# Cross attentions in slots: the first scores one slot sooner, another order in the slots, moves shared anew, fewer waits on TensorE

## The reference, cut to what matters

```python
q = _split_heads(query @ Wq.T + bq)
k = _split_heads(key @ Wk.T + bk)
v = _split_heads(value @ Wv.T + bv)
scores = jnp.einsum('bhqd,bhkd->bhqk', q, k) / jnp.sqrt(jnp.float32(DEPTH))
scores = scores + mask * jnp.float32(-1000000000.0)
weights = jax.nn.softmax(scores, axis=-1)
ctx = jnp.einsum('bhqk,bhkd->bhqd', weights, v)
ctx = ctx.transpose(0, 2, 1, 3).reshape(query.shape[0], -1, D_MODEL)
return ctx @ Wo.T + bo
```

## Time and profile before

| | us |
|---|---|
| median of 3 runs (lowest, highest) | 2327.14 (2322.26, 2331.49) |
| profiled execution, its own time | 2325.12 |
| its span | 2323.3 |
| granted TensorE clock, mean of the span | 0.944 |
| TensorE busy, whole span | 2062.7 (89%) |
| VectorE, ScalarE, GpSimd busy | 1335.3, 1105.0, 459.7 |
| stage D from 1293.87 to 2065.80 (771.93): TensorE, VectorE, ScalarE, GpSimd busy | 741.43, 476.33, 402.31, 214.06 |
| ScalarE's moves (line 636), mean of one | 0.595 |
| VectorE's moves (line 746), mean of one | 0.685 |

### The profile page before, as it was taken

One profiled execution on the slowest core, in us unless ns is written; L12 is line 12 of the kernel. 1 busy time (PEld: TensorE's weight loads), 2 busy tenths in 40 slices (PEclk: granted clock), 3 DMA queues, 4 the chain that ended last, 5 costly groups with the idle time before them and its releaser, 6 DMA issues. The chain is left out here.

```text
span 2323.3 us, 59919 instructions
## 1 busy us (share of the span) xinstructions
PE 2062.7 (89%) x25136; PEld 1575.4 (68%) x25136; DVE 1335.3 (57%) x3546; ACT 1105.0 (48%) x2109; POOL 459.7 (20%) x367
## 2 busy tenths in 40 slices
PE   6999999999999985588997899999999999987874
PEld 4777777777777763267995677777777777764553
DVE  3566666566666656935114366666666666563685
ACT  4555555555554543521333554555455554551681
POOL 3111122221111100210001333222233332200010
PEclk9999999999999997797998999999999999996867
DMA  4111111111111001003653221122111111100000
GB/s 127 30 30 30 30 30 40 39 41 30 30 30 30 7 2 55 1 9 127 218 200 99 53 53 44 45 53 61 44 53 47 52 44 45 31 2 22 1 1 25
DMA packets 68668, 110.93 MB, mean 48 GB/s; under 512 B 14505, under 2 KB 37170, under 8 KB 68402
## 3 DMA queue, kind: packets, MB, share of 16 engines
q1 hardware_dynamic: 68402, 107.10, 15.7%
HBM read 106.04 MB, written 1.05 MB: 46 GB/s over the span
## 5 line engine op out<-in xcount | busy, mean ns | idle before, releaser
L718 DVE CUSTOM_DVE_ANT_0 maps_d<-scores_d,mask_scaled_d 128x512 f32<-128x512 f32 (+1 forms) x512 | 263.5, 571 | 217.3 <-PE scores_d L519 217.3
L718 DVE CUSTOM_DVE_ANT_0 maps_a<-scores_a,no_mask_a 128x512 f32<-128x512 f32 (+1 forms) x512 | 263.5, 571 | 214.0 <-PE scores_a L519 214.0
L529 PE MATMUL turn_a<-const,maps_a 128*128 128x128 f32 (+1 forms) x1664 | 258.7, 282 | 16.5 <-DVE mapsT_a L746 15.7
L529 PE MATMUL turn_d<-const,maps_d 128*128 128x128 f32 (+1 forms) x1664 | 258.8, 282 | 16.2 <-DVE mapsT_d L746 15.4
L636 ACT ACTIVATE mapsT_d<-turn_d 128x512 f32<-128x512 f32 x224 | 129.6, 595 | 231.8 <-PE turn_d L529 231.7
L636 ACT ACTIVATE mapsT_a<-turn_a 128x512 f32<-128x512 f32 x224 | 129.6, 595 | 231.2 <-PE turn_a L529 231.1
L529 PEld LDWEIGHTS turn_a<-const,maps_a 128*128 128x128 f32 (+1 forms) x1664 | 184.0, 142 | 74.2 <-issue 25.1
L529 PEld LDWEIGHTS turn_d<-const,maps_d 128*128 128x128 f32 (+1 forms) x1664 | 184.1, 142 | 74.0 <-issue 25.1
L641 ACT ACTIVATE maps_a<-maps_a,neg_max_a 128x1024 f32<-128x1024 f32 (+1 forms) x256 | 222.5, 953 | 1.9 <-DVE neg_max_a L725 1.9
L641 ACT ACTIVATE maps_d<-maps_d,neg_max_d 128x1024 f32<-128x1024 f32 (+1 forms) x256 | 222.5, 953 | 1.9 <-DVE neg_max_d L725 1.9
L746 DVE COPY mapsT_a<-turn_a 128x512 f32<-128x512 f32 x192 | 129.8, 685 | 76.7 <-PE turn_a L529 76.3
(11 more groups left out here) (412 smaller groups left out, 4396.8 us busy)
## 6 DMA issues: line engine op xcount, KB each, us to landing
w_c<-in_L_ffn_W SPq DMA_DIRECT2D x30, 1024.0 KB, 6.8
raw_a<-in_ctxT SPq DMA_DIRECT2D x48, 512.0 KB, 3.7
raw_d<-in_ctxT SPq DMA_DIRECT2D x48, 512.0 KB, 3.7
mask_scaled_d<-in_mask SPq DMA_DIRECT2D x32, 400.2 KB, 5.4
raw_a<-in_ctxT SPq DMA_DIRECT2D x16, 65.0 KB, 3.0
raw_d<-in_ctxT SPq DMA_DIRECT2D x16, 65.0 KB, 7.0
x<-in_x SPq DMA_DIRECT2D x1, 1024.0 KB, 5.4
Wk_c_b<-in_L_attn_Wk_c SPq DMA_DIRECT2D x1, 1024.0 KB
```

What stands on the lines that cost most here:

```text
L529: ins = nc.tensor.transpose(TP[at % 2][0:r, P * j:P * j + P], maps[g % 2][:, j, P * t:P * t + r], chip.ident)
L718: nc.vector.tensor_tensor_reduce(maps[b][:, j, cols], SC[j][:, 0:w], mf[m % 2][:, cols] if masked else none[:, 0:w], 1.0, NEG, ALU.add, AL ...
```

## The change

It moves the scores of chunk 0 one slot ahead, from slot 0 of half g (for g+1) to slot 12 of half g (for g+2), so the first ones, (1, 0), run before half 0. VectorE's maxima of chunk 0 move with them and wait only until the tiles of the old rows that they overwrite are turned. The sums go from slot 9 to 10, and there before the k unit. The last v unit of a half goes from 12 or 9 to 11. VectorE moves tiles 7 to 10 (BY_DVE), ScalarE the others, with the copies of k and v units of the same slots; ScalarE's exponentials stay behind slot 6 and now stand before its move of tile 11. TensorE leaves out waits where another wait of its list has already covered them.

```diff
--- before.py
+++ after.py
@@ -265,10 +265,12 @@
 
 GROUPS = HALVES * NB
 K_AT = {1: 0, 4: 1, 7: 2, 10: 3}
-V_AT = [{3: 0, 6: 1, 9: 2, 12: 3}, {3: 4, 6: 5, 9: 6}]
-ROUND_AT = {0: 0, 2: 1, 4: 2, 6: 3}
-SUM_AT = 9
-LATE = 7
+V_AT = [{3: 0, 6: 1, 9: 2, 11: 3}, {3: 4, 6: 5, 11: 6}]
+ROUND_AT = {2: 1, 4: 2, 6: 3}
+NEXT_ROUND_AT = KT - 1
+SUM_AT = 10
+BY_DVE = range(7, 11)
+BY_ACT = [t for t in range(KT) if t not in BY_DVE]
 FIRST = [("n", 0, 0), ("n", 0, 1), ("q", 0, 0), ("k", 0, 0), ("k", 0, 1), ("v", 0, 0), ("k", 0, 2), ("v", 0, 1),
          ("v", 0, 2), ("k", 0, 3), ("v", 0, 3), ("v", 0, 4), ("v", 0, 5), ("v", 0, 6), ("q", 1, 0), ("k", 0, 4),
          ("k", 0, 5), ("k", 0, 6), ("k", 0, 7), ("n", 1, 0), ("n", 1, 1), ("q", 0, 1), ("q", 1, 1)]
@@ -292,10 +294,13 @@
 def round_order():
 
     order = [("score", 0, c, j) for c in range(4) for j in range(4)]
+    order += [("score", 1, 0, j) for j in range(4)]
     for g in range(GROUPS):
         for t in range(KT):
             if t in ROUND_AT and g + 1 < GROUPS:
                 order += [("score", g + 1, ROUND_AT[t], j) for j in range(4)]
+            if t == NEXT_ROUND_AT and g + 2 < GROUPS:
+                order += [("score", g + 2, 0, j) for j in range(4)]
             if t == SUM_AT and g:
                 order.append(("sums", g - 1))
     order.append(("sums", GROUPS - 1))
@@ -371,10 +376,10 @@
 
             if at >= 0:
                 g, t = at // KT, at % KT
-                if t < LATE:
-                    eng.wait_ge(moved_act, LATE * g + t + 1)
+                if t in BY_DVE:
+                    eng.wait_ge(moved_dve, len(BY_DVE) * g + t - BY_DVE.start + 1)
                 else:
-                    eng.wait_ge(moved_dve, (KT - LATE) * g + t - LATE + 1)
+                    eng.wait_ge(moved_act, len(BY_ACT) * g + BY_ACT.index(t) + 1)
 
         def key_columns(chunk):
             return slice(BANK * chunk, BANK * chunk + even(chunk))
@@ -486,7 +491,8 @@
             def k_unit(m, k):
 
                 chunk, h, bank = k % 4, k // 4, bank_of(("k", m, k))
-                pe.wait_ge(ctx_ready, 4 * m + chunk + 1)
+                if h == 0:
+                    pe.wait_ge(ctx_ready, 4 * m + chunk + 1)
                 wait_bank(("k", m, k))
                 for c in range(HALVES):
                     cols, outs = key_columns(chunk), slice(P * h, P * h + P)
@@ -497,7 +503,8 @@
             def v_unit(m, u):
 
                 bank = bank_of(("v", m, u))
-                pe.wait_ge(ctx_ready, 4 * m + u // 2 + 1)
+                if m == 0:
+                    pe.wait_ge(ctx_ready, u // 2 + 1)
                 wait_bank(("v", m, u))
                 for t in range(2 * u, min(2 * u + 2, KT)):
                     cols = slice(P * t, P * t + rows(t))
@@ -512,7 +519,8 @@
                 m, h, w = g // 2, g % 2, cross.width(chunk)
                 if chunk == 0:
                     pe.wait_ge(q_ready, m + 2 if m or h else 1)
-                wait_kept(pe, ("k", m, 4 * h + chunk))
+                if g == 0:
+                    wait_kept(pe, ("k", m, 4 * h + chunk))
                 after(pe, score_free, ROUND["score", g, chunk, 0])
                 for j in range(4):
                     own = slice(PW * j, PW * j + PW)
@@ -524,7 +532,8 @@
                 at, r = KT * g + t, rows(t)
                 if t in (0, CUT // P):
                     pe.wait_ge(exp_done, 8 * g + (4 if t == 0 else 8))
-                wait_moved(pe, at - 2)
+                if t and t % 2 == 0:
+                    wait_moved(pe, at - 2)
                 for j in range(4):
                     ins = nc.tensor.transpose(TP[at % 2][0:r, P * j:P * j + P], maps[g % 2][:, j, P * t:P * t + r],
                                               chip.ident)
@@ -543,9 +552,10 @@
                 at, r, m, h = KT * g + t, rows(t), g // 2, g % 2
                 if t == 0:
                     after(pe, out_kept, g)
-                if h == 0 and t % 2 == 0:
+                if h == 0 and t % 2 == 0 and m == NB - 1:
                     wait_kept(pe, ("v", m, t // 2))
-                wait_moved(pe, at)
+                if t % 2 or t == KT - 1:
+                    wait_moved(pe, at)
                 for a in range(2):
                     for j in range(4):
                         ins = nc.tensor.matmul(OUT[PW * j:PW * j + PW, h, T * a:T * a + T],
@@ -593,6 +603,7 @@
                     scores(0, ROUND_BEHIND[unit])
             pe.wait_ge(set_up, 2 if masked else 3)
             pe.wait_ge(project_free, len(FIRST))
+            scores(1, 0)
             for g in range(GROUPS):
                 m, h = g // 2, g % 2
                 for t in range(KT):
@@ -601,12 +612,14 @@
                     turn(g, t)
                     if t in ROUND_AT and g + 1 < GROUPS:
                         scores(g + 1, ROUND_AT[t])
+                    if t == NEXT_ROUND_AT and g + 2 < GROUPS:
+                        scores(g + 2, 0)
+                    if t == SUM_AT and g:
+                        spread_sums(g - 1)
                     if t in K_AT and m + 1 < NB:
                         k_unit(m + 1, 4 * h + K_AT[t])
                     if t in V_AT[h] and m + 1 < NB:
                         v_unit(m + 1, V_AT[h][t])
-                    if t == SUM_AT and g:
-                        spread_sums(g - 1)
                     if t and t % 2 == 0:
                         values(g, t - 2)
                         values(g, t - 1)
@@ -690,7 +703,10 @@
                     keep_v(a, b)
             for g in range(GROUPS):
                 m, h = g // 2, g % 2
-                for t in range(LATE):
+                for t in BY_ACT:
+                    if t == BY_DVE.stop and g + 1 < GROUPS:
+                        for i in range(8):
+                            exp(g + 1, i // 4, i % 4)
                     move(g, t)
                     if t == 0 and g:
                         keep_out(g - 1)
@@ -698,9 +714,6 @@
                         keep_k(m + 1, 4 * h + K_AT[t])
                     if t in V_AT[h] and m + 1 < NB:
                         keep_v(m + 1, V_AT[h][t])
-                if g + 1 < GROUPS:
-                    for i in range(8):
-                        exp(g + 1, i // 4, i % 4)
             keep_out(GROUPS - 1)
 
         @block.vector
@@ -712,8 +725,8 @@
                 if chunk == 0 and j == 0:
                     if masked and g % 2 == 0:
                         dve.wait_ge(mask_ready, m + 1)
-                    after(dve, turned, KT * (g - 1))
                 if j == 0:
+                    after(dve, turned, KT * (g - 2) + min(BANK // P * (chunk + 1), KT))
                     dve.wait_ge(scored, 4 * g + chunk + 1)
                 nc.vector.tensor_tensor_reduce(
                     maps[b][:, j, cols], SC[j][:, 0:w], mf[m % 2][:, cols] if masked else none[:, 0:w], 1.0, NEG,
@@ -797,19 +810,24 @@
             for s in v:
                 nc.vector.memset(s[:, :, 16:32], 1.0).then_inc(set_up, 1)
             dve.wait_ge(bias_ready, BIASES)
+            for j in range(4):
+                largest(1, 0, j)
             for g in range(GROUPS):
                 m, h = g // 2, g % 2
                 for t in range(KT):
-                    if t >= LATE:
+                    if t in BY_DVE:
                         move(g, t)
+                    if t == NEXT_ROUND_AT and g + 2 < GROUPS:
+                        for j in range(4):
+                            largest(g + 2, 0, j)
                     if t in ROUND_AT and g + 1 < GROUPS:
                         for j in range(4):
                             largest(g + 1, ROUND_AT[t], j)
                         if ROUND_AT[t] == 3:
                             negate(g + 1)
-                    if t >= LATE and t in K_AT and m + 1 < NB:
+                    if t in BY_DVE and t in K_AT and m + 1 < NB:
                         keep_k(m + 1, 4 * h + K_AT[t])
-                    if t >= LATE and t in V_AT[h] and m + 1 < NB:
+                    if t in BY_DVE and t in V_AT[h] and m + 1 < NB:
                         keep_v(m + 1, V_AT[h][t])
                     if t == SUM_AT and g:
                         finish(g - 1)
```

## The result

| | before | after |
|---|---|---|
| median (lowest, highest), us | 2327.3 (2322.26, 2331.49), 4 runs | 2234.73 (2226.17, 2235.96), 4 runs |
| profiled execution, its own time; span | 2325.12; 2323.3 | 2235.69; 2233.9 |
| one pair of halves | 51.50 | 48.53 |
| stage A, D: first turn to output projection | 811.14, 811.64 | 764.62, 764.63 |

The ratio is 0.9595, 95% interval 0.9564 to 0.9626: 92.6 us less in medians, 89.4 in the two spans. The forecast was 2238 and a pair of 48.7.

The account below looks back on a forecast made before the run. TensorE's own work and its stalls bound the kernel. Stalls of 2.67 us per pair plus 0.15 of switches gave 2.8, with the ends 88 us over two stages: 2238 us, own range 2225 to 2250, overall 2205 to 2264.

Parts of the forecast that it names:

- Slot 2: Scores of chunk 1 wait for VectorE's maxima of chunk 0, 0.50 us in both halves; 1.00 per pair goes.
- turn 12: Turn 12 waits for VectorE's move of tile 10, queued behind finish; 0.54 + 0.68 = 1.22 us per pair goes.
- the odd half's end: Last three values units, 1.21 us against 0.81, and some 0.05 at the turn before; 0.45 per pair goes.
- the remnant at slot 10: Even half's k unit waits for the copy of slot 9's v unit; about 0.25 us, which stays.
- The switches: Changed order of TensorE's units makes switches between them cheaper; net 0.15 us per pair, bounds 0 and 0.3.
- ScalarE's new work: Moves 11 and 12 and slot 11's v copy, behind the exponentials, end in time by 0.3 us or more.
- The waits left out: 52 TensorE waits per pair, taken as costing 0; upper bound 52 x 51 ns = 2.65 us per pair.
- The equal values units: Two values units take 0.65 us with or without a wait before them, so met waits cost nothing measurable.
- The ends: First and last halves of each stage: 0.5 us less, about 2 gained; stage 43.5 to 44, two stages 88.
- Another wait in each half's place: Rival: ScalarE's queue or the maxima run 0.5 us over in each half; 2268 us, chance 0.12.
- The sums bank: Rival: scores at slot 12 wait for finish's reciprocal to read their bank; slower, 2349 us, chance 0.04.
- The price of the waits: Rival: waits themselves cost TensorE, half the bound, 1.3 us per pair, 40 us more gained; 2198, chance 0.09.

Follow-up runs that it names:

- e3: Kernel before with only the scores of chunk 0 and their maxima moved to slot 12 of the half before; 2285.00 us, ratio 0.9831.
- e4: Changed kernel with the scores of chunk 0 back at slot 0, all else as changed; 2293.03 us, ratio 0.9865.
- e5: Changed kernel with the sums, and so VectorE's finish, back at slot 9; 2312.94 us, ratio 0.9944.
- e6: Changed kernel with move 10 and the k copy of slot 10 given to ScalarE too; 2285.43 us, ratio 0.9826.
- e2: Changed kernel with all 52 left-out waits per pair put back; 2231.45 us, ratio 0.9598.
- e1: Kernel before with only the 52 waits per pair left out; 2316.67 us, ratio 0.9962.
- e10: Changed kernel run once more, nothing altered; 2232.89 us, ratio 0.9594 against the kernel before.
- e11: Kernel before with four more waits, met long ago, ahead of the scores of slot 2; 2322.92 us, ratio 0.9984.

## Why the prediction was right

**The stalls.** All four were read rightly from distances of start to start. Slot 2 (1.00), turn 12 (1.22) and the odd half's end (0.45) went; the remnant at slot 10 stayed at 0.23 where 0.25 was said. e3 and e4 take them away one group at a time; e5 brings a stall at slot 11 back (1.95 a pair, 0.81 and 1.14), through finish in VectorE's queue, as the prediction had it.

**The switches** were the term that was too small: 0.15 a pair was taken, 0.30 came (2.97 less 2.67). Turn 1 to k unit costs 0.36 where the working used the pair of turn and k unit at 1.90, measured 1.84 now, twice a pair: 0.11 of the missing 0.15. Where sums now precede the k unit, the place that the prediction had no row for, nothing was gained: turn 10, sums and k unit took 1.04 in the even half before and after. The rest is hundredths. The stated bounds were 0 and 0.3, so this came at their edge. Over thirty halves that made 43.9 us of a forecast 41.5.

**ScalarE's new work** was covered as said; the single-tile copy took 0.37 and the cover of move 12 was 0.81, where 0.3 or more was said. e6 gives the margin: one move and one copy more is too many by 1.56 in odd halves.

**The waits left out** were taken as free. e2 shows that they are in the changed kernel. In the kernel before they were not quite (e1, 6 to 8 us). The bound of 2.65 us a pair was twice too high, as only 26 of the 52 were instructions (e1). The gain is in the 1.00 of slot 2 already, since it was part of the stall. The equal values units were the right witness for met waits and said nothing on unmet ones. The Trainium skill, "Perfetto Trace Analysis", Sequencer-only Instruction, was weighed for the other end. Its hidden tail shows here only behind an unmet wait (0.09 us more with the 51 ns instruction than without); behind met ones it shows nowhere. Its statement that the profiled time leaves the wait out holds for the row L91 above, which stays at 51 ns with the wait for the maxima unmet, and does not hold for the row L521: 2.9 us for an instruction that holds the same wait and a met one.

**The ends.** From the first turn on, the two stages gave 46.5 and 47.0 us. The forecast had 43.5 to 44 each, 88 in all. Before stage A's first turn 3.3 were lost: 1.07 for scores (1,0), and the rest the start-up, which differs from one execution to another (first turn at 61.89, and at 59.99 in e10). The clock differs there too: from 48 to 60 the granted clock was 0.72 in this profile, and 0.86 in those of the kernel before and of e10; what that costs isn't shown.

93.5 - 3.3, and 0.7 gained between the stages and 1.5 lost behind stage D, is 89.4, the difference of the spans. With the 1.07 of scores (1,0) taken off in each stage, as the forecast did, the stages gave 91.4 for its 88, and 2.0 lost outside them, in no term of the working, brought that back to 89.4: that the time came within 3.3 us of the forecast is in part luck. Half 30 lost most of its wait at slot 2 (turn to scores 0.68 and not 2.43) but waited for ScalarE at values 11, as the prediction had said.

**The rivals.** Another wait in each half's place (2268) did not come; e6 shows its mechanism, ScalarE's queue, alive one move away. The sums bank (2349) did not come either, and no run made it bite: the reciprocal ended 1.05 us ahead. e5 puts finish sooner, so it is the old stall again and not this rival. The price of the waits (2198, 40 us) came at a fifth of that, and only in the kernel before.

## What to carry to other kernels

Compare each step of a repeated pattern, start to start, with the same step where it isn't held up: the sum of the differences forecast the two stages' gain as 88 us where 93.5 came, where idle time alone would have shown two thirds of it. When an engine at half load makes the bound engine wait, look for the one long piece of work in its queue ahead of the short urgent one, and move the long one behind; here undoing that order costs 80 us, 9 of them by the clock, and ScalarE's own block of 7 us set how much it could take over. Waits that are met cost nothing measurable on TensorE in these kernels; drop or regroup them only ahead of a stall that can't be removed.

## What the runs showed of the hardware that was not expected

- From the release to the first matmul TensorE took 0.15 us when the unmet wait was an instruction of its own ahead of a weight load with another wait, 0.10 when that instruction carried two waits and the load had one (e11), 0.06 when the load itself carried it (e1). The 51 ns of an instruction of its own ran behind the release in the first case.
- The profiled time of such an instruction can hold its wait: 2.77 to 3.30 us in e11, while it was 51 ns for the same wait in the kernel before.
- The granted clock fell to 1.2 GHz for 3.4 us, three times a stage, in a kernel (e5) with TensorE busy 96% of its stages (737.75 of 765.60 us); the stretch before it had TensorE busy 2.04 of 3.00 us, and the same stretch of an ordinary half, with 2.05 of 3.00, kept 2.4 GHz. In the changed kernel it fell 1.1 us behind the wait of 2.73 in half 30.
